# Routed rows of a mixture of experts: loaded in feature quarters and turned by VectorE in 32x32 squares, in place of TensorE's transposes

## The reference

```python
xf = x.reshape(N, 256)                       # N = 4096 tokens
shared = new_gelu(xf @ Wfc_s + bfc_s) @ Wproj_s + bproj_s
probs = softmax(xf @ Wr)                     # 8 experts
topk_p, topk_i = top_k(probs, 2)             # two experts for each token
gate[token, topk_i] = topk_p / sum(topk_p)
for e in range(8):                           # Wfc[e] 256x1024, Wproj[e] 1024x256
    h = new_gelu(xf @ Wfc[e] + bfc[e]) @ Wproj[e] + bproj[e]
    routed = routed + h * gate[:, e:e + 1]
return shared + routed
```

## Time and profile before

| what | value |
|---|---|
| median of 3 runs | 950.82 us |
| the profiled execution's own time | 949.33 us |
| its span, first to last instruction | 947.6 us |
| granted TensorE clock, mean | 0.995 of full speed |
| busy: TensorE | 907.5 us, 96% |
| busy: VectorE, ScalarE, GpSimd | 63%, 55%, 36% |
| routed stage | 525 to 939 us of the span, 35 blocks |

### The profile page before, as it was taken

The page is one execution under the profiler, slowest core; times in us unless marked ns, Lnnn a source line. Parts: engine busy times, 40 slices in busy tenths (PEclk is TensorE's granted clock), DMA queues, the critical chain, the costliest instruction groups (busy, mean ns, idle before and its releaser), DMA issues.

```text
span 947.6 us, 20435 instructions
## 1 busy us (share of the span) xinstructions
PE 907.5 (96%) x7038; PEld 799.6 (84%) x7039; DVE 593.5 (63%) x1433; ACT 521.9 (55%) x1057; POOL 339.2 (36%) x318
## 2 busy tenths in 40 slices
PE   6999999999998999999999999999999999999996
PEld 4688985566664778888889899999999999999996
DVE  4988787667756766666656556565464656565452
ACT  3684424565545734447554657565575756575552
POOL 3567223111202255455555134233242423332222
PEclk9999999999999999999999999999999999999998
DMA  9300020000002011111125553325243432522222
GB/s 255 105 1 1 1 90 1 1 2 1 1 1 97 2 70 70 70 49 70 70 82 179 178 143 109 71 40 140 46 125 54 126 54 43 137 44 47 46 46 34
DMA packets 48944, 64.01 MB, mean 68 GB/s; under 512 B 9985, under 2 KB 41921, under 8 KB 48769
## 3 DMA queue, kind: packets, MB, share of 16 engines
q0 software_dynamic: 17504, 34.87, 15.7%
q1 hardware_dynamic: 31248, 27.46, 9.9%
q10 hardware_dynamic: 144, 1.05, 0.3%
HBM read 38.59 MB, written 24.77 MB: 67 GB/s over the span
## 4 chain that ended last, share of the span: by engine, by line
PE 77%; DVE 7%; ACT 3%; issue 3%; POOL 1%; DMA 1%; SPq 0%; DVEq 0%; POOLq 0%; ACTq 0%
PE PS L135 22%; PE PS L136 21%; PE PS L137 21%; PE PS L867 3%; DVE mxpad L1128 2%; PE PS L898 2%; PE PS L1816 2%; PE PS L912 2%; PE PS L918 1%; ACT recs L1026 1%; DVE hidl L141 1%; POOL routed_rows L1545 1%; ACT prT L1007 1%; DVE mxT L1139 1%; PE PS L839 0%
## 5 line engine op out<-in xcount | busy, mean ns | idle before, releaser
L1862 ACT ACTIVATE hideh<-PS,be 128x256 fp32r<-128x256 f32 x280 | 139.4, 498 | 152.1 <-PE PS L137 147.4
L1890 POOL DMA_INDIRECT out_rows<-y,toki x70 | 124.1, 1774 | 264.4 <-DVE y L1930 254.6
L141 DVE TENSOR_TENSOR hidel<-act32e,hideh 128x256 fp32r<-128x256 f32 x280 | 118.4, 425 | 107.1 <-ACT act32e L1864 96.3
L135 PE MATMUL PS<-xTeh,wfch 128*128 128x256 f32 x560 | 159.4, 285 | 1.8 <-issue 1.1
L137 PE MATMUL PS<-xTeh,wfcl 128*128 128x256 f32 x560 | 158.4, 283 | 0.0
L136 PE MATMUL PS<-xTel,wfch 128*128 128x256 f32 x560 | 158.4, 283 | 0.0
L135 PE MATMUL PS<-wprh,hideh 128*128 128x256 f32 x560 | 157.8, 282 | 0.0
L137 PE MATMUL PS<-wprh,hidel 128*128 128x256 f32 x560 | 154.8, 276 | 0.0
L136 PE MATMUL PS<-wprl,hideh 128*128 128x256 f32 x560 | 154.8, 276 | 0.0
L1864 ACT ACTIVATE act32e<-PS,be 128x256 f32<-128x256 f32 x280 | 139.4, 498 | 3.0 <-DVE hidel L141 3.0
L135 PEld LDWEIGHTS PS<-xTeh,wfch 128*128 128x128 f32 x560 | 107.3, 192 | 3.5 <-issue 2.6
(11 more groups left out here) (275 smaller groups left out, 2094.3 us busy)
## 6 DMA issues: line engine op xcount, KB each, us to landing
xr<-routed_rows SPq DMA_DIRECT2D x36, 272.0 KB
fcraw<-in_Wfc POOLq DMA_DIRECT2D x8, 1024.0 KB
prraw<-in_Wproj POOLq DMA_DIRECT2D x8, 1024.0 KB
X<-in_x SPq DMA_DIRECT2D x8, 512.0 KB, 6.2
out_rows<-X SPq DMA_DIRECT2D x8, 512.0 KB, 3.0
routed_rows<-pads SPq DMA_DIRECT2D x8, 272.0 KB
out_rows<-y,toki POOLq DMA_INDIRECT x70
ctx<-in_ctxT SPq DMA_DIRECT2D x4, 256.0 KB, 6.7
```

What stands on the lines that cost most here:

```text
L135: nc.tensor.matmul(out, wh, xh, start=first, stop=False)
L141: return eng.tensor_tensor(out, whole, high.bitcast(F32), ALU.subtract)
L1862: nc.scalar.activation(hid[0][:, j, :], PS[:, j % 4, 0:BLK], ACT.Gelu_apprx_tanh, bias=bias)
L1890: nc.gpsimd.indirect_dma_start(out=out, out_offset=bass.IndirectOffsetOnAxis(ap=toki[:, h:h + 1], axis=0), in_=y[:, h, :], in_offset=None, ...
```

## The change

- SyncE loads the 256 rows with four DMAs, one for each quarter of the features (64 of them): quarter q goes to partitions 32q to 32q+31, and row t*32+j stands on partition 32q+j in slot t (tile `xb`, 8 slots of 64 features). A fifth DMA loads the meta to `metar`.
- VectorE turns `xb` into `xt` with one `transpose` instruction that swaps rows and columns within each 32x32 square (128 x 512 numbers). After it partition 32q+c holds features 64q+32k+c of all 256 rows. The rows of Wfc are put in the matching order on the host.
- ScalarE's `x_high` and VectorE's low part read `xt` from SBUF, with a rearranged access pattern.
- TensorE's four transposes of each block are gone.
- In `one` VectorE does the turn after the wait for `y_sent`, `gate` and `toki`, and before `take`. `xr_free` is raised by the turn. The rows of block 0 are turned by VectorE in front of its `take`, and the first increment of `xr_free` moves there.
- GpSimd's wait for the first rows counts all five DMAs.

```diff
+            X_IN = 16 * (P // SQ + 1)
...
-                sp.dma_start(xr[:], rg[0].rearrange("p h c -> p h c")).then_inc(x_in, 16)
+                for q in range(P // SQ):
+                    sp.dma_start(xb[q * SQ:(q + 1) * SQ],
+                                 rgx[0, :, :, q * KD * SQ:(q + 1) * KD * SQ]).then_inc(x_in, 16)
+                sp.dma_start(metar[:], rg[0, :, :, D:ROW]).then_inc(x_in, 16)
...
-                    if b == B - 1:
-                        routed_first()
...
                     def load(g, e, par, i):
                         sp.wait_ge(xr_free, g + 1)
-                        sp.dma_start(xr[:].rearrange("p (a h) c -> p a h c", a=1),
-                                     rg[bass.ds(e * NBR + i, 1)].rearrange("a p h c -> p a h c")).then_inc(x_in, 16)
+                        row = bass.ds(e * NBR + i, 1)
+                        for q in range(P // SQ):
+                            sp.dma_start(xb[q * SQ:(q + 1) * SQ].rearrange("p (a t) c -> p a t c", a=1),
+                                         rgx[row, :, :, q * KD * SQ:(q + 1) * KD * SQ].rearrange(
+                                             "a j t c -> j a t c")).then_inc(x_in, 16)
+                        sp.dma_start(metar[:].rearrange("p (a h) c -> p a h c", a=1),
+                                     rg[row, :, :, D:ROW].rearrange("a p h c -> p a h c")).then_inc(x_in, 16)
...
-                def transposes(pe, g):
-                    pe.wait_ge(x_in, g * 16 + 16)
-                    if not isinstance(g, int):
-                        pe.wait_ge(xT_ready, g)
-                    for k in range(KD):
-                        for h in range(2):
-                            last = nc.tensor.transpose(PS[:, 4, k * BLK + h * P:k * BLK + (h + 1) * P],
-                                                       xr[:, h, k * P:(k + 1) * P], ident[:])
-                    last.then_inc(x_psum, 1)
+                def first_turn(dve):
+                    dve.sem_inc(xr_free, 1)
+                    turn(dve, 0)
+
+                def turn(dve, g):
+                    dve.wait_ge(x_in, g * X_IN + X_IN)
+                    nc.vector.tensor_copy(meta[:], metar[:])
+                    nc.vector.transpose(xt[:].rearrange("p t k j -> p (t k j)"),
+                                        xb[:].rearrange("p t c -> p (t c)")).then_inc(xr_free, 1)

                 def take(dve, g):
-                    dve.wait_ge(x_psum, g + 1)
                     dve.wait_ge(xT_high, g + 1)
-                    low(nc.vector, xTp[1][:].rearrange("p k n -> p (k n)"), PS[:, 4, :],
-                        xTp[0][:].rearrange("p k n -> p (k n)")).then_inc(xT_ready, 1)
-                    nc.vector.tensor_copy(meta[:], xr[:, :, D:ROW]).then_inc(xr_free, 1)
+                    low(nc.vector, squares(1), xt[:].rearrange("p t k j -> p k t j"),
+                        squares(0)).then_inc(xT_ready, 1)
...
-                        transposes(pe, g + 1)
...
                     def x_high(g):
-                        act.wait_ge(x_psum, g + 1)
-                        nc.scalar.activation(xTp[0][:].rearrange("p k n -> p (k n)"), PS[:, 4, :],
+                        act.wait_ge(xr_free, g + 2)
+                        nc.scalar.activation(squares(0), xt[:].rearrange("p t k j -> p k t j"),
                                              ACT.Copy).then_inc(xT_high, 1)
...
                             low(nc.vector, hid[1][:, j, :], act32[:, j % 2, :], hid[0][:, j, :]).then_inc(l_ready, 1)
-                        dve.wait_ge(xr_free, g + 2)
                         dve.wait_ge(y_sent, g + 1)
                         nc.vector.tensor_copy(gate[:], meta[:, :, bass.ds(e, 1)].rearrange("p h a -> p (h a)"))
                         nc.vector.tensor_copy(toki[:], meta[:, :, E]).then_inc(gate_ready, 1)
                         dve.wait_ge(gate_ready, g + 1)
+                        turn(dve, g + 1)
                         take(dve, g + 1)
...
-                    dve.sem_inc(xr_free, 1)
```

More of the change, by code:

```diff
@@ L47, in build @@
     BLK = 2 * P
+    SQ = 32
     ROOM = N + BLK
@@ L1280, in build @@
             first_rows = Place(win_at + 4096)
-            xr = first_rows("xr", [P, 2, ROW])
+            xb = first_rows("xb", [P, BLK // SQ, KD * SQ])
+            metar = first_rows("metar", [P, 2, ROW - D])
             x_in, = phase_sems(ctx, "d_x_in")
             rg = RG.rearrange("(n h p) c -> n p h c", h=2, p=P)
+            rgx = RG.rearrange("(n t j) c -> n j t c", t=BLK // SQ, j=SQ)
+            X_IN = 16 * (P // SQ + 1)
             wr = early("wr", [P, KD, E])
@@ L1304, in build @@
             hid = [tm("hid" + n, [P, KH, L], F32R) for n in "hl"]
+            rows_at = tm.at
             rows = tm("rows", [P, TB, ROW])
@@ L1335, in shared_sync, with shared_tensor @@
                 sp.wait_ge(scattered, 16 * 2 * TB * B)
-                sp.dma_start(xr[:], rg[0].rearrange("p h c -> p h c")).then_inc(x_in, 16)
+                for q in range(P // SQ):
+                    sp.dma_start(xb[q * SQ:(q + 1) * SQ],
+                                 rgx[0, :, :, q * KD * SQ:(q + 1) * KD * SQ]).then_inc(x_in, 16)
+                sp.dma_start(metar[:], rg[0, :, :, D:ROW]).then_inc(x_in, 16)
                 for b in range(B - 2, B):
                     store(b)
-            def shared_tensor(pe, routed_first):
+            def shared_tensor(pe):
                 def transposes(b):
@@ L1565, in shared_gpsimd @@
                 pool_wait(pool, e_low, 2)
-                pool_wait(pool, x_in, 16)
+                pool_wait(pool, x_in, X_IN)
                 load_weights(pool, 1)
@@ L1771, in routed_stage @@
                 gated = tm("gated", [P, 2, D])
-                (x_psum, xT_ready, xr_free, h_psum, h_ready, y_psum, y_read, bias_gated, gate_ready,
-                 added, y_sent, b_in, xT_high, l_ready, be_ready) = phase_sems(c, """d_x_psum d_xT_ready d_xr_free d_h_psum
+                (xT_ready, xr_free, h_psum, h_ready, y_psum, y_read, bias_gated, gate_ready,
+                 added, y_sent, b_in, xT_high, l_ready, be_ready) = phase_sems(c, """d_xT_ready d_xr_free d_h_psum
                     d_h_ready d_y_psum d_y_read d_bias_gated d_gate_ready d_added d_y_sent d_b_in
@@ L1806, in routed_sync, with squares @@
                     load(before + count, E - 1, 1, 0)
-                    sp.wait_ge(x_in, (before + count) * 16 + 16)
+                    sp.wait_ge(x_in, (before + count) * X_IN + X_IN)
                     sp.sem_inc(sp_waits, 1)
-                def transposes(pe, g):
-                    pe.wait_ge(x_in, g * 16 + 16)
-                    if not isinstance(g, int):
-                        pe.wait_ge(xT_ready, g)
-                    for k in range(KD):
-                        for h in range(2):
-                            last = nc.tensor.transpose(PS[:, 4, k * BLK + h * P:k * BLK + (h + 1) * P],
-                                                       xr[:, h, k * P:(k + 1) * P], ident[:])
-                    last.then_inc(x_psum, 1)
+                xt = Place(rows_at)("xt", [P, BLK // SQ, KD, SQ])
+                def squares(n):
+                    return xTp[n][:].rearrange("p k (t j) -> p k t j", j=SQ)
+                def first_turn(dve):
[6 more added lines that the diff above has]
+                                        xb[:].rearrange("p t c -> p (t c)")).then_inc(xr_free, 1)
                 def take(dve, g):
-                    dve.wait_ge(x_psum, g + 1)
                     dve.wait_ge(xT_high, g + 1)
-                    low(nc.vector, xTp[1][:].rearrange("p k n -> p (k n)"), PS[:, 4, :],
-                        xTp[0][:].rearrange("p k n -> p (k n)")).then_inc(xT_ready, 1)
-                    nc.vector.tensor_copy(meta[:], xr[:, :, D:ROW]).then_inc(xr_free, 1)
+                    low(nc.vector, squares(1), xt[:].rearrange("p t k j -> p k t j"),
+                        squares(0)).then_inc(xT_ready, 1)
                 def routed_tensor(pe):
@@ L1934, in one @@
                             low(nc.vector, wpr[1][:, 1 - par], prraw[:], wpr[0][:, 1 - par]).then_inc(e_low, 1)
-                    dve.sem_inc(xr_free, 1)
                     dve.sem_inc(l_ready, 2)
                     every_block(dve, one)
-                return (routed_sync, routed_tensor, routed_scalar, routed_gpsimd, routed_vector), transposes, take
-            routed, first_transposes, first_take = routed_stage()
+                return (routed_sync, routed_tensor, routed_scalar, routed_gpsimd, routed_vector), first_turn, take
+            routed, first_turn, first_take = routed_stage()
             with nc.Block() as block:
@@ L1953, in _ @@
                 def _(pe):
-                    shared_tensor(pe, lambda: first_transposes(pe, 0))
+                    shared_tensor(pe)
                     routed[1](pe)
@@ L1968, in _, with routed_first @@
                 def _(dve):
-                    shared_vector(dve, lambda: first_take(dve, 0))
```

(7 more changed lines are left out.)

## The result

The changed kernel takes 965.62 us (median of 4 runs, 964.74 to 967.08), the kernel before 950.93 us in the same session (4 runs, 950.70 to 955.33). The ratio is **1.0145**, 95% interval 1.0113 to 1.0177: slower, by 14.7 us.

What follows compares the result with a forecast made beforehand. TensorE was taken to bound the kernel (77% of the last chain). Losses from late blocks, less gains in free blocks, summed to +9.7 us on 949.33, 959.0; the median's 1.5 more gave 960.5 us, range 947 to 974.

Steps and rivals of the forecast that it cites:

- The chain behind `gate`: From VectorE's `gate` to finished transposed rows, through the turn, ScalarE's copy and the low part: 2.59 us instead of 0.95.
- T: Time of VectorE's turn of 512 columns: taken as 0.69 us, bounded by 0.49 and 1.22.
- The first block's shift: In each expert's first block, VectorE's weight split, y, the scatters and the next `y_sent` come 1.66 us later.
- The second block: In each expert's second block, `gate` comes at 702.48 and the transposed rows at 705.07, so TensorE stalls 2.20 us.
- The third block: `gate` at 715.04 and transposed rows at 717.63, against 715.39 before: +2.24 us over an expert's first three blocks.
- The DMA term: Row load in small pieces while weights load, DMA engines full: about 0.5 us more, bounds 0 and 2.
- Expert 0: Same pattern as later experts, plus VectorE waiting for a second row load that lands 2 to 3 us later: +3.1 us.
- what the transposes were worth: Four transposes between TensorE's up and down projections take 0.43 us of the stream; 36 sets at most 15.5 us.
- The slope in T: Effect of the turn's time on the whole kernel: about 15 us per us of turn.
- Of the rivals, the first: GpSimd's first scatter escapes its collision with VectorE's wprl, 1.76 us saved seven times: 948.2 us, not slower; chance 0.13.
- The third (terms cancel): Turn of 0.49 us, no extra DMA time, no added loss at the start: 953 us, 951 with shorter handovers; chance 0.10.
- The second: Turn of 1.22 us gives 968.5 us; 1.5 us more DMA time on six blocks gives 977; chance 0.18.

Runs made afterwards that it cites:

- Experiment A: Changed kernel with VectorE's turn moved ahead of the wait for `y_sent` and the meta copy moved behind `gate`: 955.15 us, ratio 1.0052 against the kernel before.
- Experiment C: Changed kernel with each block's features loaded in one DMA of 1 KB pieces, so turned numbers are not the wanted ones: 959.34 us, ratio 1.009.
- experiment D: Changed kernel with a second turn of the same rows, into a spare tile, right ahead of the first: 972.56 us, ratio 1.0229 against the kernel before.
- F: Changed kernel with the turn between hidden tiles 5 and 6, meta copied to a second tile, rows issued ahead of the weights: 942.94 us, ratio 0.991.
- E: Changed kernel with the turn between hidden tiles 5 and 6 and features in one DMA, without the quarter layout: 945.63 us, ratio 0.9931.
- B: Changed kernel with the turn moved between the low parts of hidden tiles 5 and 6, load still in four parts: 969.64 us, ratio 1.0198.

## Why the prediction was right, and which sizes were off

The forecast of 960.5 us with a range of 947 to 974, slower, held; the time was 5.1 us above it. By its own steps:

- **The chain behind `gate`: right.** The turn took 0.70 us (T was set at 0.69, from the row of a subtraction of the same shape), ScalarE's gap 0.70, and `gate` to TensorE 2.70 against 2.59. The grouped lines of the loop after:

```profile
L1836 DVE STREAM_TRANSPOSE xt<-xb 128x512 f32<-128x512 f32 x35 | 24.7, 704 | 0.0
L142 DVE TENSOR_TENSOR xTel<-xt,xTeh 128x512 fp32r<-128x512 f32 x35 | 24.2, 693 | 24.4 <-ACT xTeh L1871 24.4
L1871 ACT ACTIVATE xTeh<-xt 128x512 fp32r<-128x512 f32 x35 | 22.1, 632 | 82.4 <-DVE xt L1836 82.4
```

  The estimate of 1.24 us, scaled from the Trainium skill (VectorE: DVE Perf Modes, The three transpose paths), was too high: the measurement decides, 704 ns for 128x512 in fp32.
- **The first block's shift: right.** `gate` of the second block came 22.17 us after its expert's start (711.34 - 689.17) against 20.50 before (700.82 - 680.32), +1.67, forecast 1.66; in experts 1 to 6 it is +1.5 to +2.0. Experiment A shows the cause: the turn moved ahead of the wait takes away most of the loss.
- **The second block: right in length, partly wrong in reason.** It is 13.3 to 13.4 us long (13.9 in expert 1), forecast 11.23 + 2.20 = 13.43. But only 0.30 of the stall stands before line 136 of the next block. The larger part is inside the up projection, where TensorE waits for ScalarE's act32, which I had said would add nothing by itself:

```profile
706.30 0.38 PE L136 MATMUL PS<-xTeh,wfch 128*128 128x256 f32 x1 [1.16 <-ACT act32e L1880]
```

  The two overlap, and the total is set by `gate`, so the sum came out. The sign that the prediction named, a gap of 2.2 us before line 135, is not there; the gate that comes late by 1.67 is.
- **The third block: a term too small.** In expert 3 `gate` to `gate` is 13.00 us against 12.06 before, over six experts 12.85 against 12.05 in the mean. The DMA term is thus 0.8, not 0.5, inside its bounds of 0 to 2. Experiment C takes most of it away (12.16), and the kernel wins 5 to 6 us. The Trainium skill's rule on pieces under 512 bytes (DMA: Bandwidth & Descriptors, its table's line on the minimum transfer for line rate), by which I had estimated a sum some 3 us higher, would be a term of 1.0; the 0.7 to 0.8 measured lie between that and mine. C measures the piece size and the number of DMAs together and does not part them, and no run shows what the engines do with a small piece.
- **Expert 0: the number right, in part by luck.** It grew by 3.3 us, forecast 3.1. The late rows are there: VectorE waits 1.67 us for them (537.00). But in block 1, which is 15.70 us long against 11.66, TensorE stands still for 1.72 us at 546.45 and then makes 16 steps of 0.213 us at a granted clock of 0.50 (547.3 to 550.7). That is about 1.5 us which the sum doesn't have. In experiment A the same stall of 1.72 us is followed by 0.12 us steps, and the block is 14.42 us long.
- **The mis-sized step: what the transposes were worth.** The prediction read 0.43 us per set off the seam in the earlier trace rows and assumed the rest of the stream unchanged. The runs show 0.25 (11.66 to 11.41). The sum counted 15 blocks at 0.43 (8 free ones, two of expert 6, five of the last), so the difference of 0.18 makes 2.7 us. The first three blocks of experts 1 to 5 grew by 2.69 us in the mean where 2.24 was forecast, 2.2 us in all: 0.25 of the 0.45 is `gate` to `gate`, 0.11 the chain behind it. With the start (0.6), expert 0 (0.2) and the tail below (0.9) that is 6.6, which is what the span ended above the forecast sum.
- **The slope in T** was put at 15 and is 11 to 13 (experiment D), which matters for the rivals only.
- **A term left out: the tail.** The last expert should have gained 2.15, and this stretch gained 0.3. Its first four blocks gave 1.0 (927.02 - 880.29 = 46.73 against 942.66 - 896.91 = 45.75). From the start of the last block to the end of the span it took 0.7 us more. GpSimd's last two scatters, before and then after:

```profile
937.45 1.55 POOL L1890 DMA_INDIRECT out_rows<-y,toki  x1 [7.38 <-DVE y L1930]
...
940.17 1.55 POOL L1890 DMA_INDIRECT out_rows<-y,toki  x1 [1.17 <-DVE y L1930]
```

```profile
954.39 1.55 POOL L1906 DMA_INDIRECT out_rows<-y,toki  x1 [8.01 <-DVE y L1946]
956.25 1.55 POOL L1906 DMA_INDIRECT out_rows<-y,toki  x1 [0.30 <-issue]
```

  The chain behind `gate` delays the first half of y as well, so the first scatter comes 1.3 us later in its block (954.39 - 942.66 = 11.73 against 937.45 - 927.02 = 10.43) and the second queues behind it. In F, with the turn out of that chain, the second scatter has its old place, 1.6 us after the last matmul.

Of the rivals, the first did not come about: the scatter that runs beside wprl took 3.21 us and the next started 3.52 after it, much as in the earlier trace rows. The third (terms cancel) failed on the DMA term and the ceiling. The second had a part of its cause: the DMA share was 0.3 us dearer for each expert, not 1.5, and the turn was not dearer.

## What to carry over

Before an operation moves to an engine with time to spare, ask what it will stand behind there. Here the change cost 14.7 us in a kernel that TensorE bounds. Moving 0.7 us of VectorE out from behind a wait for GpSimd's stores gave back some 9 us of it (A), a load in one piece alone 5 to 6 (C), and the earlier turn and that load together some 20 (E). The same work placed earlier, with its load issued ahead of the large one, made the kernel 0.9% faster than before (interval 0.7 to 1.1%). A wait that costs nothing today (18 us) is the first place to look. What an operation costs in a saturated stream is the length of a whole block with and without it, not the gap at the place where it stands.

## What the runs showed of the hardware

- The same stream of alternating weight loads and 256-column matmuls runs at 0.113, 0.118 or 0.120 us per step at a granted clock of 1.00, and removing four transposes moved the down projection from the first to the second. The changed kernel, without transposes, still runs at 0.113 in blocks that stalled inside the up projection (708.31 to 709.11).
- After a stall of about 3 us TensorE ran for some 6 us at 0.213 us per step (724.66 to 730.2 in B, granted clock 0.50), so that this stall cost nearly twice its length. The length of the stall alone does not decide it: behind one of 2.82 us (776.30 in B) the clock stayed at 1.00, and behind one of 1.72 us in the changed kernel (546.45) it fell to 0.50. Behind that kernel's stalls of 1.2 and 1.3 us (706.30, 727.04) the steps stayed at 0.11 to 0.12.
- 272 KB of rows (four DMAs of 64 KB and one of 16) issued beside 2 MB of weights were ready some 8 us after their last issue, with the DMA engines full. Issued 3 us sooner, ahead of the weights (F), they held nobody up in experts 1 to 6.
- A VectorE turn of 128x512 fp32 in 32x32 squares takes as long as a subtraction of that shape (704 and 693 ns).
